# A causal-attention and mixture-of-experts layer: far scores and far maxima as one-head products on the two halves of the array's rows

## The reference, cut to what matters

```python
h = _layernorm(x) * (1 + ca) + sa
q, k, v = (split_heads(h @ W + b) for W, b in ...)
rel = jnp.einsum('bhid,pd->bhip', q, rel_key)              # rel_key: [512, 16]
rel_idx = jnp.clip(j - i + p - 1, 0, p - 1)                # p = 512
logits = where(j <= i, (q . k + rel[rel_idx]) * scale, -inf)
x = x + ga * (softmax(logits) @ v @ Wo + bo)
h = _layernorm(x) * (1 + cb) + sb
x = x + gb * moe_ffn(h)                                    # top 2 of 8 experts, 3 layers each
```

## Time and profile before

| | us |
|---|---|
| timed, median of 3 runs | 3788.45 (3782.03 to 3789.36) |
| span of the profiled execution | 3677.7 |
| TensorE busy in the span | 3300.8 (90%) |
| VectorE | 2377.2 (65%) |
| ScalarE | 1463.3 (40%) |
| GpSimd | 1392.7 (38%) |

### The profile page before, as it was taken

One profiled execution on the slowest core, in us unless ns is written; L12 is line 12 of the kernel. 1 busy time (PEld: TensorE's weight loads), 2 busy tenths in 40 slices (PEclk: granted clock), 3 DMA queues, 4 the chain that ended last, 5 costly groups with the idle time before them and its releaser, 6 DMA issues. The chain is left out here.

```text
span 3677.7 us, 164235 instructions
## 1 busy us (share of the span) xinstructions
PE 3300.8 (90%) x72736; PEld 2859.8 (78%) x72736; DVE 2377.2 (65%) x4756; ACT 1463.3 (40%) x1765; POOL 1392.7 (38%) x1575
## 2 busy tenths in 40 slices
PE   6867999999999999999999999999999999379980
PEld 4546888888888888888888888888888887368770
DVE  8864667776366777744667777356676771466774
ACT  3631233445513333454233344522333445345551
POOL 5664433223364332224533322355332311222556
PEclk8988999999999999999999999999999999699995
DMA  4863101001311100104101000231110000544654
GB/s 127 242 182 90 36 25 39 30 17 30 100 55 44 38 23 26 30 17 121 47 31 39 31 27 21 63 92 45 31 31 17 29 10 13 172 133 145 193 179 146
DMA packets 243353, 254.63 MB, mean 69 GB/s; under 512 B 99496, under 2 KB 186380, under 8 KB 242524
## 3 DMA queue, kind: packets, MB, share of 16 engines
q1 hardware_dynamic: 222204, 202.68, 18.4%
q0 software_dynamic: 20448, 41.45, 3.7%
HBM read 151.36 MB, written 92.59 MB: 66 GB/s over the span
## 5 line engine op out<-in xcount | busy, mean ns | idle before, releaser
L958 DVE TENSOR_TENSOR att_acc<-att_pm,att_acc 128x512 f16<-128x512 f32 x1920 | 1262.7, 686 | 487.9 <-PE att_pm L1065 245.4
L1038 ACT ACTIVATE att_pt<-att_ps 128x1024 f32<-128x1024 f32 x560 | 574.0, 1025 | 1372.4 <-PE att_ps L1068 1372.4
L1065 PE MATMUL att_ps<-att_qx,table_x 68*128 68x64 f16 x8960 | 722.7, 194 | 0.0
L1068 PE MATMUL att_ps<-att_qz,table_z 128*128 128x64 f16 x8960 | 719.9, 194 | 0.0
L1041 ACT ACTIVATE att_pt<-att_ps 128x1024 f32<-128x1024 f32 x528 | 515.4, 1022 | 401.3 <-PE att_ps L1076 400.0
L149 POOL TENSOR_TENSOR att_qx<-att_qe,mask_i 64x1024 f16<-64x1024 f16 x128 | 239.5, 1888 | 1027.9 <-PE att_po L1159 985.6
L1068 PEld LDWEIGHTS att_ps<-att_qz,table_z 128*128 128x128 f16 x8960 | 616.2, 99 | 0.0
L1065 PEld LDWEIGHTS att_ps<-att_qx,table_x 68*128 68x128 f16 x8960 | 613.6, 99 | 0.0
L1159 PE MATMUL att_po<-att_pt,att_vn 128*32 128x128 f32 x17408 | 595.6, 278 | 0.2 <-ACT att_pt L1038 0.2
L1159 PEld LDWEIGHTS att_po<-att_pt,att_vn 128*32 128x32 f32 x17408 | 447.1, 110 | 83.3 <-issue 67.7
L1061 PE MATMUL att_ps<-att_qs,att_kn 113*128 113x64 f16 x8960 | 449.9, 194 | 34.9 <-DMA att_qs<-s_m 34.9
(11 more groups left out here) (211 smaller groups left out, 3951.7 us busy)
## 6 DMA issues: line engine op xcount, KB each, us to landing
att_qe<-s_q SPq DMA_DIRECT2D x256, 128.0 KB
moe_xs<-s_h SPq DMA_DIRECT2D x78, 256.0 KB, 3.2
s_y<-moe_y SPq DMA_DIRECT2D x78, 256.0 KB, 2.4
s_v<-att_vn SPq DMA_DIRECT2D x32, 512.0 KB, 5.2
att_vn<-s_v SPq DMA_DIRECT2D x64, 256.0 KB, 2.9
att_qs<-s_q SPq DMA_DIRECT2D x128, 66.0 KB
att_kn<-s_k SPq DMA_DIRECT2D x128, 64.0 KB, 2.3
att_x<-in_x SPq DMA_DIRECT2D x64, 128.0 KB, 6.2
```

The lines of the kernel that those rows point to most:

```text
L958: dve.tensor_tensor(held, got, held, ALU.max).then_inc(bank_done, 1)
L1038: act.activation(pt[:, k % 2, :, t * 64:t * 64 + 64].rearrange("p h (x c) -> p x h c", x=2), ps[t][:, :, :].rearrange("p x (h c) -> p x h ...
L1065: last = pe.matmul(groups[:, :, g], keep["table_x"][:, y:y + P], qx[0:G * D + G, s, x * (XQ // G) + g], start=False, stop=(g == XQ // G - ...
L1068: last = pe.matmul(groups[:, :, g], keep["table_z"][:, y:y + P], qz[:, s, x * (XQ // G) + g], start=False, stop=(g == XQ // G - 1), skip_g ...
```

## The change

`far_scores` no longer makes one product of two heads over 113 rows and 256 columns. It makes two products of one head each: rows 0 to 48 for the half e = 0, rows 64 to 112 for e = 1, 128 columns each, to two different banks. One call does four heads of each half, eight products, and fills both banks. In a score, these are the two banks of `ps[t]`. Of the maxima, the even step r waits for two free banks, fills both and signals both; the odd step r + 1 does nothing on TensorE. In the plan the odd far step gets the share of the even one before it, so that its number follows directly. VectorE still takes each bank by itself. The patterns by which VectorE and ScalarE sort the heads follow the new content of the banks.

```diff
-        line = [((at + 0.5) / len(maxima) * end, 0, at, s) for at, s in enumerate(maxima)]
+        line = [((at - (s[3] % 2 if s[0] == "far" else 0) + 0.5) / len(maxima) * end, 0, at, s) for at, s in enumerate(maxima)]
...
-                            held = acc[:, n % 2].rearrange("p (e h) c -> p h e c", e=2)[:, 2 * r:2 * r + 2]
-                            got = full[:, :].rearrange("p (h e c) -> p h e c", e=2, c=P)
+                            first_head = r % 2 * HH + r // 2 * (HH // 2)
+                            held = acc[:, n % 2, first_head:first_head + HH // 2, :]
+                            got = full[:, :].rearrange("p (h c) -> p h c", c=P)
...
-                        act.activation(pt[:, k % 2].rearrange("p (e h) c -> p h e c", e=2)[:, 4 * t:4 * t + 4],
-                                       ps[t][:, :, :].rearrange("p x (h e c) -> p (x h) e c", e=2, c=P), ACT.Exp, scale=SCALE).then_inc(p_done[t], 1)
+                        act.activation(pt[:, k % 2].rearrange("p (e h) c -> p e h c", e=2)[:, :, 4 * t:4 * t + 4],
+                                       ps[t][:, :, :].rearrange("p e (h c) -> p e h c", c=P), ACT.Exp, scale=SCALE).then_inc(p_done[t], 1)
...
-                def far_scores(bank, n, j, r):
-
-                    s, rows = n % SLOTS, 64 + KM + 1
-                    for h in range(2):
-                        last = pe.matmul(bank[:, 2 * h * P:(2 * h + 2) * P].rearrange("p (e c) -> p e c", c=P), kn[0:rows, j, 2 * r + h, :],
-                                         qs[0:rows, s, :, 2 * r + h, :], start=True, stop=True, skip_group_check=True)
+                def far_scores(banks, n, j, t):
+
+                    s, last = n % SLOTS, [None, None]
+                    for h in range(HH // 2):
+                        for e in range(2):
+                            rows, head = slice(64 * e, 64 * e + KM + 1), HH // 2 * t + h
+                            last[e] = pe.matmul(banks[e][:, h * P:(h + 1) * P], kn[rows, j, head, :], qs[rows, s, e, head, :],
+                                                start=True, stop=True, skip_group_check=True)
                     return last
 
                 def bank(number, behind, kind, n, j=0, r=0):
                     full = pm[number % NBUF]
                     b, i = divmod(n, NB)
+                    if kind == "far" and r % 2:
+                        return
                     bank_free(pe, number)
...
                     if kind == "far":
-                        last = far_scores(full[:, :], n, j, r)
+                        bank_free(pe, number + 1)
+                        first, last = far_scores([full, pm[(number + 1) % NBUF]], n, j, r // 2)
+                        first.then_inc(bank_full, 1)
...
-                    for x in range(2):
-                        if near(i, j):
+                    if near(i, j):
+                        for x in range(2):
                             last = near_scores(ps[t][:, x], kn[:, j], n, j, 2 * t + x, True)
-                        else:
-                            last = far_scores(ps[t][:, x], n, j, 2 * t + x)
+                    else:
+                        _, last = far_scores([ps[t][:, e] for e in range(2)], n, j, t)
                     last.then_inc(s_full[t], 1)
```

## The result

| | before | changed |
|---|---|---|
| median of 7 runs, us | 3788.45 (3782.03 to 3796.21) | 3828.18 (3803.44 to 3932.51) |
| ratio | 1 | 1.0094 [1.007, 1.0118] |
| span of the profiled execution | 3677.7 | 3826.1 |

The change makes the kernel slower by 40 us, where a gain of 49 was forecast. One of the seven executions, 3932.51 us at a mean granted clock of 0.803 where the others have 0.924 to 0.931, is left out of the ratio; by the ratio the loss is 36 us.

What follows compares the result with a forecast made beforehand. TensorE was taken to bound the attention. Products save 214 us, switches cost 111, leaving 103; losses of 54 behind TensorE leave 49, so 3788 - 49 = 3739 us, range 3650 to 3845.

Steps and rivals of the forecast that it cites:

- The far products: TensorE's far scores and maxima: two banks filled in 0.232 us instead of 0.435, saving 214 us over 1056 fillings.
- that rival: Rival on the far products: the two row halves don't overlap, total 3918 us; chance 0.15.
- The changes of division: TensorE switching between row halves, whole array and column quarters: 961 more switches at 0.115 us, costing 111 us.
- the rival of the free change: Rival on TensorE's switches: going between row halves and whole array costs nothing, total 3664 us; chance 0.19.
- Gain less changes: TensorE over four batches: product savings less switch costs, 66 + 24 + 13 = 103 us.
- (1) *Banks: Far maxima waiting for two free banks of three: losses of 32 us in far stages 5 to 13, 8 in near stages.
- at most some 40 us more: Sign in the changed profile: far maxima's loads wait for VectorE at most some 40 us more than now.
- VectorE catches up: Near stages: exact scores of 1.5 us between steps let VectorE catch up, so 368 x 0.02 = 8 us lost.
- Bank pairs decide: Rival on bank waits: far steps wait 0.64 us in far stages 5 to 13, 0.1 in near ones; 3838 us, chance 0.20.
- The row I rested on: Trace at 1548 to 1549: far step starts at 1549.01; needing two banks it would wait until 1549.56.
- 14 were forecast: ScalarE's exponentials in far stages 14 and 15 limit what score pairs can gain: 14 us lost.
- that sign: Condition for a wrong prediction: the clock falls in the far stretches; no size given.

Runs made afterwards that it cites:

- e3: Kernel before with only the two-bank steps for far maxima and the plan's edit, products as before: 3777.23 us, ratio 1.0247.
- e4: The changed kernel again, unaltered, in a quick session: 3693.86 us, ratio 1.0021 to the kernel before.
- e13: The changed kernel again, unaltered, in a long session: 3842.12 us, ratio 1.0123 to the kernel before.
- first run: The changed kernel as first measured and profiled, in a long session: 3828.18 us, ratio 1.0094 to the kernel before.
- e16: Changed kernel, each even far step planned at least one place behind the step before it, plan's far-score price 0.3 instead of 0.45: 3690.55 us, ratio 0.9734.
- e5: e3 with the wait for the second bank moved behind the filling of the first: 3825.0 us, ratio 1.0083.
- e7: Kernel before with far maxima taken over one head of four, the rest left out: 3740.0 us, ratio 0.9864.
- e15: e3 with each even far step planned at least one place behind the step before it: 3782.64 us, ratio 0.9968.

## Why the prediction was wrong

**Right.** The far products: 0.056 us a pair where 0.058 was said, 223 us saved where 214 was. The halves of rows overlap, so that rival is out. The changes of division: 0.093 us where 0.115 was taken from the columns' quarters, 89 us instead of 111; the rival of the free change is out. VectorE's and ScalarE's prices did not move. Gain less changes was forecast at 103 us and is 134 by these prices.

**Wrong: the step "(1) *Banks*", and in it the near stages.** It gave 40 us: 32 in far stages 5 to 13 (one step in three waits, 0.2 on average) and 8 in the near ones. e3 measures 91, and the loads wait 92 more in e4, against the sign "at most some 40 us more". TensorE's idle time ahead of far maxima grew by 39 us in the far stages of e4, near the 32, and by 65 in the near stages, where the forecast said that "VectorE catches up" and put 0.02 us a step; it is 0.18. The outcome is the one of the rival "Bank pairs decide", whose time, 3838, is 10 us from the 3828 measured. That this is so close is luck: the rival put 102 us of its waits into the far stages and 37 into the near ones, and the long session added a loss by the clock that it didn't have. Its reason was only half right, too: not VectorE's 76%, but the places. The row I rested on, a turn and two near maxima filling three banks, showed the case, and I priced it by the next maximum and by VectorE's share. What I did not do is walk through the written order and count where a two-bank step follows another step of the ring in the same place (196 of 528); I did count the division changes that way. Asking how the wait would be met with VectorE idle would have shown the round trip. And by putting the near stages at 0.02 us a step I used the mean load of VectorE for a question of neighbours.

**Too small, or missing.** ScalarE: 16 us more ahead of far scores, 14 were forecast. The clock had no term in the sum, only a mention among what would make it wrong, and that sign came: 109 us at the lower level became 160 in the quick session's traces, 15 to 25 us lost. With -223 + 89 + 91 + 16 and these the sum is -12 to -2, and +7 was measured.

**Readings.** The slices of the earlier trace rows show VectorE between 3 and 7 and ScalarE between 1 and 5 over the attention, not 2 to 7 and 2 to 6; nothing hangs on it. The sentence that the 110.75 us between span and median lie "all outside the changed work" was wrong, as said in the section on the result: the two are of different sessions.

**The size of the loss.** The change is 1.0021 in the quick session and 1.0094 and 1.0123 in long ones. In the changed kernel's traces of long sessions the lower clock holds 317 (e13) and 324 us (first run) instead of 160; 171 and 180 of them lie in far stages 5 to 13, where e4 has 27. There is no trace of before from a long session, but every timed execution has its mean granted clock. From quick to long it falls from 0.951 to 0.943 or 0.944 for before, about 65 us more at the lower level in the whole execution, and from 0.947 to 0.9235 or 0.9265 for the changed kernel, 170 to 200 us more. At most half of the difference, 50 to 65 us, covers the 30 to 40 us by which the loss is larger there. So the loss grows with the clock; why the clock gives so much less in those sessions, and less to this kernel, stays open. The spread kernel with the new price (e16) is back at 0.945.

## What to carry to other kernels

When steps begin to ask for two buffers of a small ring at once, walk through the written order and count where such a step stands next to another user of the ring: each such place can cost a round trip through the consumer, however idle that is (0.53 us each here). Move the steps apart before the change is judged; here the same edit was 1.2% slower with neighbours and 1.5% faster without, 2.7% with the planner's price lowered. A change of the array's division is a cost of its own and can be lowered by sorting the work of one kind together.

## What the runs showed of the hardware

Products of 49 rows on the two halves of the array's rows run at once, starts 3 to 4 ns apart, a pair of 128 columns each 0.056 us, loads hidden. Going from halves to the whole array or back costs 0.093 us each time.

At the lower granted clock, 64-column products start every 53 ns instead of 30, and half a weighing takes 0.85 us instead of 0.44.

The two kinds of session differ in one more visible thing beside the clock. In the traces of quick ones an exponential starts 0.04 us, at most 0.08, after the end of the last product that it waited for. In those of long ones some exponentials and maxima start 0.6 to over 2 us late: 36 to 47 maxima and 13 to 34 exponentials in a trace, each of them while one of GpSimd's 256 indirect DMAs runs or within 3 us of its end, stretches that make up 15% of the span. Timeline of all engines, the changed kernel, long session:

```profile
1611.54 0.41 PE L1062 MATMUL att_pm<-att_qs,att_kn 113*128 113x64 f16 x8
1611.78 0.40 PE L1066 MATMUL att_pm<-att_qx,table_x 68*128 68x64 f16 x8
1612.12 0.40 PE L1079 MATMUL att_pm<-att_qs,att_kn 49*128 49x128 f16 x8
1612.72 0.98 POOL L883 DMA_INDIRECT s_h<-att_h,row  x1 [0.30 <-issue]
1614.10 0.69 DVE L959 TENSOR_TENSOR att_acc<-att_pm,att_acc 128x512 f16<-128x512 f32 x1 [2.39 <-remote]
1614.31 1.02 ACT L1042 ACTIVATE att_pt<-att_ps 128x1024 f32<-128x1024 f32 x1 [4.93 <-PE att_ps L1079]
```

The bank at 1611.54 is full by about 1612.2, and VectorE takes it at 1614.10; no operation of any engine that the profile shows holds it. In sum the late starts cover 73 to 86 us of each such trace, overlaps counted once, where the sessions' times of the kernel before lie 104 us apart. The traces without the change (e5, e7, e15) have them too, so they are no effect of the change. The cause is open: the same chip number showed both kinds of session, and that GpSimd's indirect DMAs are at work each time is a coincidence in time that no run has separated.
